# Keys and values projected from split contexts, with GpSimd splitting each context at the end of a batch

## What is computed

```
q = layernorm(x) @ w_q.T + b_q;  k = ctx @ w_k.T + b_k;  v = ctx @ w_v.T + b_v      # 16 heads of 16
out = softmax(q k^T / 4) @ v;  x = x + tanh(g_xattn) * (out @ w_o.T + b_o)
for each token: its 2 best experts by bid;  expert(x) = (silu(x @ gate) * (x @ up)) @ down
x = x + tanh(g_ffn) * (weighted sum of the two experts of layernorm(x))
```

## Time and profile before

| what | value |
|---|---|
| median of 3 runs | 1199.79 us |
| lowest, highest | 1197.14, 1202.40 us |
| the profiled execution | 1202.42 us |
| its span, first to last instruction | 1200.6 us |
| mean granted TensorE clock | 0.961 of full |
| busy: PE, PEld, DVE, ACT, POOL | 91%, 75%, 56%, 46%, 26% |

### The profile page before, as it was taken

The page is one execution under the profiler, slowest core; times in us unless marked ns, Lnnn a source line. Parts: engine busy times, 40 slices in busy tenths (PEclk is TensorE's granted clock), DMA queues, the critical chain, the costliest instruction groups (busy, mean ns, idle before and its releaser), DMA issues. The chain is left out here.

```text
span 1200.6 us, 24032 instructions
## 1 busy us (share of the span) xinstructions
PE 1091.6 (91%) x8213; PEld 896.2 (75%) x8213; DVE 668.0 (56%) x1588; ACT 555.3 (46%) x891; POOL 315.6 (26%) x366
## 2 busy tenths in 40 slices
PE   5789999999999988289899999999989999999994
PEld 4456666666666655247599999999849999999994
DVE  2546777777777774365644444444564444444442
ACT  3456676666676664155533333333453333333331
POOL 2122444444343332311311122112221122112111
PEclk8899999999999997589999999999999999999998
DMA  8100111111111101384621121112141122112111
GB/s 297 52 15 24 39 37 44 48 46 37 37 37 37 44 30 48 121 317 164 220 56 32 22 36 32 28 30 36 31 140 28 22 36 36 31 23 36 32 26 23
DMA packets 48025, 72.85 MB, mean 61 GB/s; under 512 B 6256, under 2 KB 42864, under 8 KB 44912
## 3 DMA queue, kind: packets, MB, share of 16 engines
q0 software_dynamic: 16896, 43.53, 14.2%
q1 hardware_dynamic: 30000, 27.68, 7.8%
q10 hardware_dynamic: 1088, 1.11, 0.3%
HBM read 47.14 MB, written 24.90 MB: 60 GB/s over the span
## 5 line engine op out<-in xcount | busy, mean ns | idle before, releaser
L1519 POOL DMA_INDIRECT out<-y,token x64 | 104.6, 1634 | 473.1 <-DVE y L1453 364.1
L1379 ACT ACTIVATE silu<-gate 128x512 f32<-128x512 f32 x128 | 76.5, 597 | 277.4 <-PE up L1287 277.4
L1299 PE MATMUL down<-w_split,h_hi 128*128 128x512 f32 x512 | 185.9, 398 | 0.0
L901 DVE TENSOR_REDUCE max_neg<-maxps 128x4 f32<-128x1024 f32 x128 | 156.4, 1222 | 52.8 <-PE maxps L510 51.1
L1287 PE MATMUL gate<-x_hi,w_split 128*128 128x256 f32 x1024 | 184.5, 282 | 0.0
L1287 PE MATMUL up<-x_hi,w_split 128*128 128x256 f32 x1024 | 183.8, 281 | 0.0
L1444 DVE TENSOR_TENSOR h<-silu,up 128x512 f32<-128x512 f32 x128 | 88.0, 688 | 171.4 <-ACT silu L1379 171.4
L703 ACT ACTIVATE probs<-scores 128x1024 f32<-128x1024 f32 x124 | 127.8, 1030 | 60.5 <-PE scores L535 60.5
L1287 PEld LDWEIGHTS gate<-x_hi,w_split 128*128 128x128 f32 x1024 | 148.8, 188 | 3.0
L1287 PEld LDWEIGHTS up<-x_hi,w_split 128*128 128x128 f32 x1024 | 147.8, 188 | 0.0
L1301 PE MATMUL down<-w_split,h_lo 128*128 128x256 f32 x512 | 144.2, 282 | 0.0
(11 more groups left out here) (164 smaller groups left out, 1756.3 us busy)
## 6 DMA issues: line engine op xcount, KB each, us to landing
xg<-dispatched SPq DMA_DIRECT2D x41, 272.0 KB, 2.8
stage<-gate_T POOLq DMA_DIRECT2D x8, 1024.0 KB, 7.5
stage<-up_T POOLq DMA_DIRECT2D x8, 1024.0 KB, 9.4
stage<-down_T POOLq DMA_DIRECT2D x8, 1024.0 KB, 12.0
x_all<-x SPq DMA_DIRECT2D x16, 256.0 KB, 6.3
ctxT<-ctxT SPq DMA_DIRECT2D x16, 256.0 KB, 2.7
out<-x_all SPq DMA_DIRECT2D x16, 256.0 KB, 2.1
out<-y,token POOLq DMA_INDIRECT x72, 3.8
```

The lines of the kernel that those rows point to most:

```text
L901: V.tensor_reduce(to, maxps[:], AX.X, ALU.max, negate=True).then_inc(s["max_taken"], 1)
L1299: mm(down[t][:].rearrange("p (n d) -> p n d", n=2), h_hi[:, i, rows], split[:, :, cols], start=i == 0, stop=False, skip_group_check=True)
L1379: nc.scalar.activation(silu[pair % 2][:], gate[pair % 2][:], ACT.Silu).then_inc(s_silu, 1)
L1519: pool.indirect_dma_start(out, bass.IndirectOffsetOnAxis(token[:, t:t + 1], axis=0), y[:, t, :], None, compute_op=ALU.add).then_inc(s_adde ...
```

## The change

The keys and values of the batches in the loop are no longer made from fp32 operands. The context and the two weight matrices are each split into a high part (a cast to fp32r) and the rest (what the cast lost, again fp32r), and each projection becomes high by high, high by rest and rest by high, summed in PSUM: twelve fp32r matmuls in place of four fp32 ones. This holds for the keys of batches 4 to 15 and the values of batches 3 to 15; the earlier ones stay as they were.

- VectorE splits the two weight matrices once, after maxima 6 and 7 of batch 0, ahead of the batch loop (`split_weights`); TensorE waits for both (`w_split`) before body 0.
- GpSimd splits one context per batch (`split_ctx`), the one of batch b+3, as its last work of body b. In body 1 it splits two.
- SyncE loads the context of b+3 in body b, where it loaded that of b+2; an input of 17 contexts (the last one twice) serves the loads.
- Eight more tiles of 2 KB per partition lie in SBUF.

```diff
--- before.py
+++ after.py
@@ -147,6 +147,10 @@
         wk_s = sb("wk_s", [P, HC, D])
         wv_s = sb("wv_s", [P, HC, D])
         wo_s = sb("wo_s", [P, HC, D])
+        w_high = {what: sb(f"w{what}_high", [P, HC, D], f32r) for what in "kv"}
+        w_rest = {what: sb(f"w{what}_rest", [P, HC, D], f32r) for what in "kv"}
+        c_high = [sb(f"ctx_high{i}", [P, HC, SEQ], f32r) for i in range(2)]
+        c_rest = [sb(f"ctx_rest{i}", [P, HC, SEQ], f32r) for i in range(2)]
         bq_s = sb("bq_s", [P, HC])
         bk_s = sb("bk_s", [P, HC])
         bv_s = sb("bv_s", [P, D])
@@ -225,7 +229,7 @@
             ln2_done bias_added q_split k_split high_chain unit_written unit_read first_loaded picks_loaded picks_ready half_made shifted max_scored max_taken pv_done pv_read
             sums_inverted x2_stored sigmoid_half_ready route_chain masks_ready second_ready
             rows_chain rows_ready scattered count_chain counted values_made
-            scale_chain scale2_chain""".split()
+            scale_chain scale2_chain ctx_high_made ctx_split w_high_made w_split""".split()
         s = {n: sem(n) for n in names}
         misc_read = [sem(f"misc_read{n}") for n in range(MISC)]
 
@@ -425,9 +429,15 @@
 
             def body(b, par, use, ahead, nxt, back, late):
 
-                if ahead:
+                if isinstance(b, int) and ahead:
                     sp.wait_ge(s["misc_written"], use.before)
                     load_ctx(b + 2, par)
+                    if b == 1:
+                        use.written(sp, "V")
+                        load_ctx(b + 3, 1 - par)
+                elif ahead:
+                    sp.wait_ge(s["ctx_split"], b - 1)
+                    load_ctx(b + 3, 1 - par)
                 if back:
                     store_residual(b - 1, use)
                 if nxt:
@@ -476,6 +486,27 @@
                 for t in range(QT):
                     for c in range(HC):
                         last = mm(use.bank("V")[:, t, :], cT[par][:, c, t * P:(t + 1) * P], wv_s[:, c, :], start=c == 0, stop=c == HC - 1)
+                last.then_inc(s["misc_written"], 1)
+
+            def three_terms(high, rest, high2, rest2):
+                return [(l, r, c) for l, r in ((high, high2), (high, rest2), (rest, high2)) for c in range(HC)]
+
+            def project_k_in_parts(b, par, use):
+                pe.wait_ge(s["ctx_split"], b - 2)
+                use.free(pe, "K")
+                terms = three_terms(w_high["k"], w_rest["k"], c_high[par], c_rest[par])
+                for o in range(HC):
+                    for n, (l, r, c) in enumerate(terms):
+                        last = mm(use.bank("K")[:, o, :], l[:, c, o * P:(o + 1) * P], r[:, c, :], start=n == 0, stop=n == len(terms) - 1)
+                last.then_inc(s["misc_written"], 1)
+
+            def project_v_in_parts(b, par, use):
+                pe.wait_ge(s["ctx_split"], b - 2)
+                use.free(pe, "V")
+                terms = three_terms(c_high[par], c_rest[par], w_high["v"], w_rest["v"])
+                for t in range(QT):
+                    for n, (l, r, c) in enumerate(terms):
+                        last = mm(use.bank("V")[:, t, :], l[:, c, t * P:(t + 1) * P], r[:, c, :], start=n == 0, stop=n == len(terms) - 1)
                 last.then_inc(s["misc_written"], 1)
 
             def write_unit(n):
@@ -626,8 +657,10 @@
                     if ahead:
                         stack(b + 2, what[0], int(what[1]), unit(b, what))
 
-                if nxt:
+                if isinstance(b, int) and b < 2:
                     project_v(1 - par, use)
+                elif nxt:
+                    project_v_in_parts(b + 1, 1 - par, use)
                 max_of_next(0)
                 if back:
                     turn_heads(b - 1, 0, use)
@@ -635,8 +668,10 @@
                 if back:
                     turn_heads(b - 1, 1, use)
                 max_of_next(1)
-                if ahead:
+                if isinstance(b, int) and ahead:
                     project_k(b + 2, par, use)
+                elif ahead:
+                    project_k_in_parts(b + 2, par, use)
                 score(b, par, 1)
                 max_of_next(2)
                 if ahead:
@@ -675,6 +710,7 @@
                     logits(use)
                 stack_ahead("Q1")
 
+            pe.wait_ge(s["w_split"], 2)
             over_batches(pe, body)
             last_batch = BATCHES - 1
             turn_heads(last_batch, 0, EPILOGUE)
@@ -886,6 +922,11 @@
                     last = V.bn_aggr(mv2[:, t, :], stats2[:, t, :])
                 last.then_inc(s["ln2_stats"], 1)
 
+            def split_weights(n, what, raw):
+                V.tensor_copy(w_high[what][:], raw[:]).then_inc(s["w_high_made"], 1)
+                dve.wait_ge(s["w_high_made"], n + 1)
+                V.tensor_tensor(w_rest[what][:], raw[:], w_high[what][:].bitcast(fp32), ALU.subtract).then_inc(s["w_split"], 1)
+
             def read_v(par, use):
 
                 use.written(dve, "V")
@@ -1001,6 +1042,8 @@
                     rest_part(1, "K")
                 if pair == 2:
                     rest_part(1, "Q")
+                if pair >= 6:
+                    split_weights(pair - 6, "kv"[pair - 6], (wk_s, wv_s)[pair - 6])
             read_maxima(0, PRO1)
 
             def body(b, par, use, ahead, nxt, back, late):
@@ -1080,6 +1123,14 @@
                 xb = x_all[:, bass.ds(b, 1)].rearrange("p o t d -> p (o t) d")
                 G.tensor_tensor(xb, xb, bo_s[:].unsqueeze(1).to_broadcast([P, QT, D]), ALU.add).then_inc(s["bias_added"], 1)
 
+            def split_ctx(c, par, use):
+
+                alone.wait_ge(s["ctx_loaded"], c * 16 + 16)
+                use.written(alone, "V")
+                G.tensor_copy(c_high[par][:], cT[par][:]).then_inc(s["ctx_high_made"], 1)
+                alone.wait_ge(s["ctx_high_made"], c - 2)
+                G.tensor_tensor(c_rest[par][:], cT[par][:], c_high[par][:].bitcast(fp32), ALU.subtract).then_inc(s["ctx_split"], 1)
+
             def split(b, what, use, units):
 
                 use.read(alone, what)
@@ -1126,6 +1177,10 @@
                     scatter(b - 2, par)
                 if ahead:
                     add_bias(b + 2)
+                if isinstance(b, int) and b == 1:
+                    split_ctx(3, 1, use)
+                if ahead and not is_first(b):
+                    split_ctx(b + 3, 1 - par, use)
 
             over_batches(pool, body)
             scale_of(BATCHES - 1, "scale2_chain", "ln2_stats", mv2, rstd2, shift2, "ln2_scaled")
@@ -1571,7 +1626,7 @@
     experts = np.arange(EXPERTS, dtype=np.float32)
     arrays = {
         "x": a(x),
-        "ctxT": np.ascontiguousarray(a(ctx_1024).transpose(0, 2, 1)),
+        "ctxT": np.ascontiguousarray(a(ctx_1024)[[*range(BATCHES), BATCHES - 1]].transpose(0, 2, 1)),
         "wq": head_columns(a(L0_xattn_w_q)),
         "wk": head_columns(a(L0_xattn_w_k)),
         "wv": np.ascontiguousarray(a(L0_xattn_w_v).T),
```

## The result

The changed kernel took **1219.49 us** (median of 4 runs, 1216.28 to 1221.72) beside 1198.88 of the kernel before on the same chip: a ratio of 1.0157, 95% interval 1.0133 to 1.0181. A second set of five runs gave 1217.97 and 1.0151 (1.0127 to 1.0175). Slower by 1.5%, where 2.3% was forecast: inside the range, but near the rival in which the clock stays up. The profiled execution took 1216.28 us, with a span of 1214.5 (before: 1200.6).

The account below looks back on a forecast made before the run. PE, 93% busy, and GpSimd's nearly as tight thread to pair 1 bound the loop. Chain 13.8 + 1.2 - 0.6 - 0.4 = +14.0, clock +14: +28.0 on 1202.42 is 1230.4, less 2.6 to the median: 1228 us, range 1208 to 1241.

Parts of the forecast that it names:

- the rival in which the clock stays up: Batch loop: GpSimd's chain late but PE's clock never falling, 1214 us (1210 to 1217); chance 0.26.
- GpSimd going from the context split into `scale_x` without a wait for `mv`: Sign in GpSimd's loop timeline that its thread is late; before, it idles 0.70 and 0.21 us ahead of `scale_x`.
- the delay returns in each period: Loop: all behind pair 1's delayed scores is late too, so bodies 3 to 13 each lose 1.05 or 1.50 us.
- the rival of about no change: PE regains the delay in short waits between pair 1 and the queries: 1200 to 1206 us; chance 0.06.
- Body 2 gains: Small term: body 2 is not delayed and gains what its second thread is early by, 0.6 us.
- 2.34 us from the end of the bias to the start of `scale_x`: GpSimd's split at a body's end: cast 0.61, subtraction 1.28, gaps of 0.15 between, ahead and behind.
- the turn of the loop: Even bodies: cost to GpSimd of the loop turn, no longer hidden in its wait; 0.47 us added, zero as other bound.
- the slack of 1.08 and 0.61: Microseconds by which GpSimd's and ScalarE's thread precedes PE at pair 1's scores, in odd and even bodies.
- the projections: PE's keys and values: twelve fp32r matmuls take 1.50 us instead of 1.92, saving 0.42 each, nearly nothing in the run.
- I take +1.2: VectorE's two weight splits ahead of body 0 lengthen the run by 1.2 us (0 to 2.6).
- seven falls in eleven bodies, +14 us: Loop: PE's idle hole before pair 1 lowers its clock, 2.0 us per fall; +14 us (0 to 27).
- the first rival: Clock stays up, all else as forecast: 1199.8 + 14.0 = 1214 us (1210 to 1217); chance 0.26.

Follow-up runs that it names:

- e3: Kernel before plus an unused GpSimd cast and subtraction of 128x512 ending bodies 1 to 13, fp32 projections kept: 1210.99 us, ratio 1.0087.
- e5: Changed kernel with GpSimd's context split moved right behind `scale_x`: 1200.38 us, ratio 1.0011 to the kernel before.
- e7: e5 with ScalarE's exponentials of pair 0 ahead of `norm_x` and the weight splits ahead of batch 0's values and maxima: 1200.85 us, ratio 1.0021.
- e4: Changed kernel with a second, unused GpSimd cast and subtraction behind the context split: 1247.51 us, ratio 1.0412 to the kernel before.
- e11: Changed kernel, split in its last place, plus 52 PE instructions that only check a long-set semaphore after attention: 1210.32 us, ratio 1.0078.
- e6: Kernel before with 22 tiny unused PE matmuls ahead of batch 0's values: 1215.29 us, ratio 1.0126.
- e9: e5 plus 92 PE instructions that only check a long-set semaphore, between attention and expert stage: 1198.29 us, ratio 0.9987 to the kernel before.
- e10: e5 plus 52 PE instructions that only check a long-set semaphore, between attention and expert stage: 1193.72 us, ratio 0.9945 to the kernel before.
- e2: Changed kernel with GpSimd's context split moved behind the split of the keys: 1209.00 us, ratio 1.0079 to the kernel before.
- e8: e7 with 42 tiny unused PE matmuls ahead of batch 0's values: 1204.16 us, ratio 1.0038 to the kernel before.
- e12: e10 with VectorE's first choice of an expert ahead of the maxima of pair 2: 1192.79 us, ratio 0.9938 to the kernel before.

## Why the prediction was right, and where it was not

**Right: the direction and the path.** GpSimd's thread decides and PE's does not. "GpSimd going from the context split into `scale_x` without a wait for `mv`", ScalarE's idle time up "to some 4 us" (3.97), PE waiting before pair 1: all are there, and e3 shows that the pair is the whole cost in the loop. That "the delay returns in each period" holds too: from the scores of pair 1 to the next queries' split it is 13.70 us before and after, so nothing of the delay is won back there, and the rival of about no change is out. Body 2 gains: it was 27.60 us and is 26.98, 0.62 less, where 0.6 was forecast.

**Mis-sized: "2.34 us from the end of the bias to the start of `scale_x`".** It is 2.05. Only one of three gaps of 0.15 is there, between the cast and the subtraction that waits for it; the cast starts 0.06 us before the bias has ended, and `rstd` 0.09 behind the subtraction. And the turn of the loop, for which 0.47 was added, costs nothing: with it and without it is 2.05. `scale_x` is late by 1.84 us in one parity and 1.35 in the other, and less the slack of 1.08 and 0.61 that is 0.76 and 0.74 at pair 1. Measured: 0.83 per body, 11 bodies, 9.2 us, against 13.8 (0.05 of the 0.83 is the step from the end of ScalarE's exponentials, 165.01, to PE's start, 165.06, which the slack left out). The zero that the prediction kept as the bound for the turn was the right value.

**Mis-sized: the projections.** 1.63 us instead of 1.50 (by its own step of 0.12 twelve matmuls take 1.44, not 1.42; that is the smaller part). From the first pair of matmuls to the second it is 0.35 us (its rows start at 157.90 and 158.25), and only then 0.24 per pair; e5 prices the two of a body at 0.6 instead of 0.84. In the changed kernel this didn't matter, as forecast.

**Mis-sized: "I take +1.2" for the weight splits.** Timeline of VectorE in the changed kernel:

```profile
41.73 0.42 DVE L926 CAST wk_high<-wk_s 128x512 fp32r<-128x512 f32 x1
42.18 0.69 DVE L928 TENSOR_TENSOR wk_rest<-wk_s,wk_high 128x512 fp32r<-128x512 f32 x1
...
44.38 0.69 DVE L928 TENSOR_TENSOR wv_rest<-wv_s,wv_high 128x512 fp32r<-128x512 f32 x1
44.99 0.41 DVE L949 CAST max_rows<-misc 16x256 fp32r<-16x256 f32 x1
```

PE's timeline at the values that open body 0:

```profile
45.12 2.92 PE L488 MATMUL misc<-wv_s,ctxT 128*128 128x256 f32 x6 [0.46 <-DVE wv_rest L928]
```

PE waits for the second split. From the start of maxima 6 (40.59) to these values it is 4.53 us; in the kernel before it is 3.79 (41.19 to 44.98), and so it is in e7, which makes the splits earlier. The cost is 0.74, on the path that was forecast.

**Failed: the clock, "seven falls in eleven bodies, +14 us".** The clock in 100 to 430 us reads 1.00, which the prediction had named as the sign that its second half is wrong. Two things led there. The hole is 1.36 us instead of "2.0 us or more", since the delay is shorter and the projections longer than I had them. And the stretch around it then holds 3.38 us of PE work, not at most 3.0; of the rows that I had to choose from, that is nearest to the one with 3.45, at which the clock stayed. The rule of the Trainium skill that the prediction weighed (TensorE: Matmul & The Clock Gate, Why this matters for your kernels) would have kept the clock up, and this trace agrees with it; e4 shows that a hole of 3.36 us does bring a fall. The price was wrong as well: a fall costs 0.74 us there, where the prediction took 2.0, so seven would have cost 5 us and not 14. The step rested on three rows and on a hole that I had estimated too long, and it carried more than half of the chance.

**Missed: the expert stage, +6 to +8 us.** No term spoke of it, because the change doesn't touch it. The forty more matmuls in PE's program were never costed for their mere number. It is nearly half of the loss. That the total came out well inside the range is thus luck: 28 us were forecast, half of them for a clock that did not fall, and 20.6 were measured, nearly half of them in a stage that the forecast left out. With the expert stage put right, e11, the change costs 10 us, 1210, at the lower edge of the range; the first rival, 1214, had 14.

**What makes up the expert stage's loss.** Stretch tables of the whole stage, PE alone: before, changed, e5, e6.

```profile
511.93:1200.60 688.67, 661.41 (x4580) 0.98 0.26 62
519.68:1214.46 694.78, 661.95 (x4580) 0.98 0.26 61
504.03:1202.25 698.22, 664.84 (x4580) 0.97 0.25 61
516.84:1213.22 696.38, 659.58 (x4580) 0.98 0.26 61
```

Length less busy time is PE's idle time: 27.3 us before, 32.8 in the changed kernel, 33.4 in e5, 36.8 in e6. Of the changed kernel's 5.6 more, the "issue" waits are 5.1; of e5's 6.1 they are all (6.3). The other 3.4 us of e5 are the same 4580 matmuls at a lower granted clock, and that belongs to the execution: e5's twelve executions have mean granted clocks from 0.952 to 0.963, and the profiled one is at 0.952. In e6 PE also waits 3.8 us longer for rows of tokens (`turned <- xg`, 17.6 against 13.8).

**Open.** That the waits depend on the place of instructions is shown by e6, e9, e10 and e11, with the loops unchanged; that it is the fetching of instructions which PE waits for is argued from that, since the profile names no releaser. All of these waits stand at one kind of place: behind an expert without further tiles, where PE branches over their code straight to the next expert's gate (`br_lt` in `over_tiles_hinted`). Behind the two experts whose further tiles are worked there is none in any of the fourteen profiles. Which places are bad was not mapped, and 52 was one hit after 92; it may be off again after any further edit of PE's program. The Trainium skill (Runtime: NRT & Kernel Launch, Instruction fetch mechanics) describes a sequencer that streams its program in blocks, with crossings mostly hidden and a stall where a taken branch leaves the blocks at hand; waits that come and go with position, and only behind a taken branch, fit its second half, but no run here shows which block was missing.

## What to carry to other kernels

Price work that is moved to an idle engine by the slack at its place in that engine's queue, not by the engine's share of busy time: the same 2.0 us split costs 0.8 us a body at the end of GpSimd's list, uses up PE's whole gain behind the keys' split, and is free behind `scale_x`. Before a small instruction of VectorE with two SBUF operands is blamed for its length, look at what GpSimd runs at that moment. And after an edit that changes the number of instructions, compare the stages that it did not touch: a version was rescued here (1.0011 to 0.9945) by 52 instructions that do nothing.

## What was not expected of the hardware

- VectorE's instructions on 128x16 with two SBUF operands last until GpSimd's running subtraction ends: 0.98 and 0.70 us instead of 0.17. Its cast does the same: in e5 one such instruction starts at 270.16, takes 0.42, and ends at 270.58 beside the keys' cast (269.95 to 270.56). The maxima, which read PSUM, run beside it at their usual time (1.23 us).
- PE can wait 0.9 to 4.2 us at a matmul for nothing that the profile shows. It happened twice in seven of the fourteen profiles (the changed kernel's two, e2, e4 to e7), once in two (e8, e9), and not at all or for 0.6 us each time in the five others (before, e3, e10 to e12); the number of its instructions ahead of that place changes it.
- A hole of 1.36 us in each body of 28.2 us left the clock at 1.00 throughout; one of 3.36 us took it down to a mean of 0.71 over the next 5 us and of 0.94 in the loop, at a price of 0.74 us per body.
- A cast of 128x512 took VectorE 0.42 us where twice the 128x256 one would be 0.58.
